# A three-stage pipeline over sixteen groups: the third stage four iterations behind the first instead of five, with a new order on every engine

## The chip, the core and the metric

The kernel runs on one core of a Trainium2 chip. The core has TensorE (PE, products and transposes), VectorE (DVE), ScalarE (ACT), GpSimd (POOL) and SyncE (SP, which issues DMAs). Each engine works through a list of its own in order, and semaphores tie the lists together. The metric is the device time of one execution in microseconds.

## What is computed

The input is 32 sequences of 256 tokens of 128 values. Three residual steps follow one another:

```python
    x = x + 0.5 * _L0_ffn_ref(_layernorm(x, axis=-1), ...)
    x = x + _L0_attn_ref(_layernorm(x, axis=-1), L0_attn_W_qkv, L0_attn_W_out)
    x = x + 0.5 * _L0_ffn_ref(_layernorm(x, axis=-1), ...)
```

The feed-forward is a mixture of eight experts (four of width 128, four of width 256). A router takes each token's two best by the sigmoid of its logits, weighs them to a sum of one, and the result is the weighted sum of `square(relu(x @ W1e)) @ W2e`. The attention is linear: `elu(q) + 1` and `elu(k) + 1` after a rotary embedding, 16 heads of 8, with one state per head and sequence:

```python
    kv = jnp.einsum('bhtd,bhtv->bhdv', k_feat, v)
    k_sum = k_feat.sum(axis=2)
    denom = jnp.maximum(jnp.einsum('bhtd,bhd->bht', q_feat, k_sum), 1e-06)
    out = jnp.einsum('bhtd,bhdv->bhtv', q_feat, kv) / denom[..., None]
```

## The kernel before, in words

**Groups, streams, chunks.** 16 groups (`NG`) of two sequences, 512 tokens each. Each group goes through three streams: `f1` (first feed-forward), `at` (attention), `f2` (second feed-forward). A feed-forward has 12 chunks (`NC`) of 128 hidden columns. A chunk is three products "up" on TensorE (`up`, L496 to L498; values are split into a high and a low part, so one product becomes three), then VectorE's relu times the root of the expert's weight (`weighted`, L1025, tile `hid`), ScalarE's square (L719) and rounded copy `h_hi` (L730), GpSimd's remainder `h_lo` (L858), and three products "down" (`down`, L514 to L516). "Up" writes two PSUM banks in turn; `hid` has six buffers.

**Iterations and places.** Every engine runs `iteration(t)` for t from -3. An iteration has 24 places. f1 of group t+1 takes places 0 to 11, one chunk each; f2 of group t+1-`SHIFT` takes places 12 to 23; a chunk's down products stand 9 places behind its up products (`DOWN_BEHIND`). Where one feed-forward is alone (`alone`), it takes every second place over 24. `SHIFT` is 5, so f1 is alone for t=-1 to 3 and f2 from the second half of t=14; between them the iterations are paired. `quarter(t, j)` on TensorE and `squares(t, j)` on ScalarE do the places 3j to 3j+2; `weighted(t, place)` on VectorE and `remainders(t, ...)` on GpSimd go by single places.

**What stands between the places.** Around the chunks each engine's `iteration` writes out by hand where the other steps go. For each stream: statistics (`stats`, `mean_variance`), the inverse deviation on GpSimd (`inv_std`), the normed input `xn` on ScalarE (`norm`, L676), its transpose on TensorE (`transpose`, L458) into PSUM bank 0, the evacuation to `xT` (`evacuate_x`, L688), high and low parts (`high_part` on VectorE, `low_part` on GpSimd, L846). `xT` is one buffer that all three streams share, and `evacuate_x` waits until the low parts of the others are made. The routers add `logits` (L477), `exp_logits` (L697, L701), the choice of two on VectorE, `root_of_weights` (L852) on GpSimd, `spread_roots` (L1003, L1009), `weight_rows` (L467, bank 0 again), `rows_of_weights` (`g_row`, L709), and SyncE's DMAs that write the rows to HBM and broadcast them into `g_all`, which `weighted` needs. `tp_free` makes TensorE wait until bank 0 is read. At a feed-forward's end ScalarE copies its sum (`copy_yT`, L741; it waits for the last down product), TensorE transposes it back (`back`, L533) and VectorE adds it to x (`add_moe`, L1033).

**Attention** is `q` and `kv` (L547), the rotary steps on VectorE (`rope_q_sin` L1044, `rope_q_cos`, `rope_q_sum`, `rope_k`, `rope_k_sum`), `exp_q`, `copy_v` (L762), `exp_k` on ScalarE, `q_features`, `k_features`, `state` (L589), `mask_state`, `attend` (L601), `normalise`, `attn_transpose` (L610), `copy_attnT` (L767), `out_proj` (L620) and `add_attention` (L1128). Before, iteration t did q and kv of group t-1 late and state to out_proj of group t-2.

Of the kernel before, what the change touches and what calls it, by code (L numbers as in the profile page):

```python
# [47 lines left out]
CQ = NC // TG  # L48
# [15 lines left out]
SHIFT = 5  # L64
# [103 lines left out]
def build(nc, x_in, wqkv, wout, router, w1, w2, const, out, rows):  # L168
    ctx = ExitStack()
    with ctx:  # L170
# [263 lines left out]
        def _(pe):  # L434
            mm = nc.tensor.matmul

            def tp_free(t, pos):

                n = [done(m + (pos > k)) for k, m in
                     enumerate((t + 2, t + 1 - SHIFT, t - 1, t + 2 - SHIFT, t + 2))]  # L440
# [4 lines left out]
                if due(n[2]):  # L445
                    pe.wait_ge(s_xT["at"], value(n[2]))
                if due(n[3]):
                    pe.wait_ge(s_ex["f2"], value(n[3]))
                if due(n[4]):
                    pe.wait_ge(s_gr["f1"], value(n[4]))  # L450
# [85 lines left out]
            def quarter(t, j, par):  # L536

                for place in range(CQ * j, CQ * (j + 1)):
# [86 lines left out]
            def iteration(t, par):  # L625
                transpose("f1", t + 2, t, 0)
                quarter(t, 0, par)
                state(t - 2)
                logits("f1", t + 2)
                quarter(t, 1, par)  # L630
                weight_rows("f2", t + 1 - SHIFT, t, 1)
                attend(t - 2)
                quarter(t, 2, par)
                transpose("at", t - 1, t, 2)
                quarter(t, 3, par)
                attn_transpose(t - 2)
                if alone("f1", t - 1):
                    back("f1", t, t - 1)
                if not alone("f2", t - 1):
                    back("f2", t - SHIFT, t - 1)  # L640
                transpose("f2", t + 2 - SHIFT, t, 3)
                quarter(t, 4, par)
                out_proj(t - 2)
                q(t - 1)
                logits("f2", t + 2 - SHIFT)
                quarter(t, 5, par)
                weight_rows("f1", t + 2, t, 4)
                quarter(t, 6, par)
                kv(t - 1, 0)
                kv(t - 1, 1)  # L650
                quarter(t, 7, par)
# [9 lines left out]
        def _(act):  # L661
# [17 lines left out]
            def evacuate_x(s, n, t, pos):  # L679
# [31 lines left out]
            def squares(t, j):  # L711

                todo = [k for place in range(CQ * j, CQ * (j + 1)) for k in chunks(t, place)]
# [57 lines left out]
            def iteration(t, par):  # L771
                n1, n2, n2_last = t + 1, t + 1 - SHIFT, t - SHIFT
                evacuate_x("f1", t + 2, t, 0)
                squares(t - 1, 7)
                norm("at", t - 1)
                exp_logits("f1", t + 2)
                squares(t, 0)
                norm("f2", t + 2 - SHIFT)
                squares(t, 1)
# [5 lines left out]
                evacuate_x("at", t - 1, t, 1)  # L785
# [452 lines left out]
```

## Time and profile before

| | us |
|---|---|
| median of 3 runs | 803.7 (803.64 to 804.73) |
| the profiled execution | 804.86 |
| its span in the trace | 803.1 |
| busy: TensorE / GpSimd | 725.4 / 686.8 |
| busy: ScalarE / VectorE | 598.4 / 582.8 |

The span is what the trace covers, from the first to the last instruction. Products overlap on TensorE and their ends are modelled, so its pace is read from starts. An idle time in brackets behind an instruction is that of its engine just before it, with what ended it.

### The profile page before, as it was taken

The numbers are of one execution on the slowest core, as the hardware profiler recorded it, in microseconds if no ns is written. First come the engines' busy times: TensorE is split into PE (matmuls) and PEld (weight loads), VectorE is DVE, ScalarE is ACT, GpSimd is POOL, SyncE is SP. The second block draws the span as 40 slices with busy tenths as digits, with TensorE's granted clock in tenths as the row PEclk, the third lists the DMA queues.
The fourth block names the chain that finished last, engine by engine and source line by source line (L and its number), as shares of the span: only waits on it lengthen the run. The fifth ranks groups of instructions, "written<-read, shape, count | busy, mean of one in ns | idle before, by whom it ended". The sixth has DMA issues, their size and how long they took to land.

```text
span 803.1 us, 13042 instructions
## 1 busy us (share of the span) xinstructions
PE 725.4 (90%) x3600; PEld 589.8 (73%) x3600; DVE 582.8 (73%) x1832; ACT 598.4 (75%) x1219; POOL 686.8 (86%) x668
## 2 busy tenths in 40 slices
PE   1779888889999999999999999999999987978987
PEld 1557666667788888888888888888887866866755
DVE  3445689787969787877878796978786768577533
ACT  3577677657787978888888888797878776656755
POOL 3778868869999999999999999999999868667865
PEclk9999899989999999999999999999999999899989
DMA  5544022033233221333323233322223311303330
GB/s 177 184 162 130 13 95 106 1 105 107 106 107 119 85 94 49 129 97 106 119 107 120 107 120 105 119 76 101 66 104 107 119 61 46 120 2 118 119 119 26
DMA packets 31159, 79.36 MB, mean 99 GB/s; under 512 B 3312, under 2 KB 14448, under 8 KB 31088
## 3 DMA queue, kind: packets, MB, share of 16 engines
q1 hardware_dynamic: 30800, 78.47, 28.9%
q8 instruction: 29, 0.48, 0.2%
q14 instruction: 42, 0.34, 0.1%
q10 hardware_dynamic: 288, 0.07, 0.1%
HBM read 73.81 MB, written 4.72 MB: 98 GB/s over the span
## 4 chain that ended last, share of the span: by engine, by line
POOL 39%; PE 21%; DVE 18%; issue 9%; ACT 8%; DMA 4%; DVEq 0%; POOLq 0%; SPq 0%; ACTq 0%
POOL h_lo L858 26%; DVE hid L1025 5%; POOL root_f L852 4%; DMA g_all_f<-rows_f 3%; PE bank L496 3%; PE bank L514 3%; POOL rstd_f L837 2%; PE bank L498 2%; PE bank L497 2%; PE bank L516 2%; PE bank L515 2%; ACT h_hi L730 2%; POOL x_lo_f L846 2%; ACT xn_f L676 2%; PE bank L589 2%
## 5 line engine op out<-in xcount | busy, mean ns | idle before, releaser
L858 POOL TENSOR_TENSOR h_lo<-hid,h_hi 128x512 fp32r<-128x512 f32 x384 | 493.5, 1311 | 79.1 <-ACT h_hi L730 78.7
L1025 DVE SCALAR_TENSOR_TENSOR hid<-bank,g_all_f 128x512 f32<-128x512 f32 x384 | 262.5, 685 | 151.3 <-PE bank L498 109.5
L719 ACT ACTIVATE hid<-hid 128x512 f32<-128x512 f32 x384 | 228.8, 622 | 52.0 <-DVE hid L1025 51.5
L730 ACT ACTIVATE h_hi<-hid 128x512 fp32r<-128x512 f32 x384 | 225.6, 620 | 4.9 <-ACT hid L719 0.8
L496 PE MATMUL bank<-x_hi_f,w_hi 128*128 128x512 f32 x384 | 166.8, 434 | 16.4 <-DVE hid L1025 15.8
L514 PE MATMUL bank<-h_hi,w_hi 128*128 128x512 f32 x384 | 156.7, 408 | 17.3 <-ACT yT L741 10.4
L498 PE MATMUL bank<-x_hi_f,w_lo 128*128 128x512 f32 x384 | 154.7, 403 | 0.0
L515 PE MATMUL bank<-h_lo,w_hi 128*128 128x512 f32 x384 | 154.0, 401 | 0.0
L497 PE MATMUL bank<-x_lo_f,w_hi 128*128 128x512 f32 x384 | 153.8, 401 | 0.0
L516 PE MATMUL bank<-h_hi,w_lo 128*128 128x512 f32 x384 | 153.6, 400 | 0.0
L496 PEld LDWEIGHTS bank<-x_hi_f,w_hi 128*128 128x128 f32 x384 | 74.4, 194 | 41.4 <-DVE hid L1025 24.9
L514 PEld LDWEIGHTS bank<-h_hi,w_hi 128*128 128x128 f32 x384 | 74.0, 193 | 39.8 <-POOL h_lo L858 14.0
L498 PEld LDWEIGHTS bank<-x_hi_f,w_lo 128*128 128x128 f32 x384 | 74.0, 193 | 18.2
L516 PEld LDWEIGHTS bank<-h_hi,w_lo 128*128 128x128 f32 x384 | 73.5, 191 | 17.1
L515 PEld LDWEIGHTS bank<-h_lo,w_hi 128*128 128x128 f32 x384 | 73.9, 192 | 16.1
L497 PEld LDWEIGHTS bank<-x_lo_f,w_hi 128*128 128x128 f32 x384 | 74.7, 195 | 11.1
L676 ACT ACTIVATE xn_f<-x_sb,nbias_f,rstd_f 128x128 f32<-128x128 f32 x128 | 52.4, 481 | 7.8 <-POOL nbias_f L839 7.8
L852 POOL TENSOR_TENSOR root_f<-cwt_f,c_half 128x8 f32<-128x8 f32 x32 | 54.6, 1706 | 0.0
L846 POOL TENSOR_TENSOR x_lo_f<-xT,x_hi_f 128x512 fp32r<-128x512 f32 x32 | 41.6, 1299 | 14.0 <-DVE x_hi_f L943 14.0
L688 ACT ACTIVATE xT<-bank 128x512 f32<-128x512 f32 x48 | 28.4, 591 | 29.0 <-PE bank L458 19.1
L943 DVE CAST x_hi_f<-xT 128x512 fp32r<-128x512 f32 x32 | 21.5, 671 | 26.8 <-ACT xT L688 26.8
L697 ACT ACTIVATE ex_f<-bank 128x32 f32<-128x32 f32 x32 | 6.3, 198 | 45.1 <-PE bank L477 45.1
(102 smaller groups left out, 1021.3 us busy)
## 6 DMA issues: line engine op xcount, KB each, us to landing
g_all_f<-rows_f SPq DMA_DIRECT2D x128, 512.0 KB, 5.5
x_sb<-in_x SPq DMA_DIRECT2D x16, 256.0 KB, 3.3
out_x<-x_sb SPq DMA_DIRECT2D x16, 256.0 KB, 7.1
g_all_f<-in_w SPq DMA_DIRECT2D x2, 768.0 KB, 6.8
con<-in_const SPq DMA_DIRECT2D x1, 584.0 KB, 6.4
rows_f<-g_row_f SPq DMA_DIRECT2D x32, 16.0 KB, 1.4
g_all_f<-in_wqkv SPq DMA_DIRECT2D x1, 192.0 KB, 6.5
con<-in_const ACTq DMA_DIRECT2D x1, 68.0 KB, 3.2
```

Source lines behind the costliest of these rows:

```text
L496: mm(o, w1_hi[:, w], x_hi[s][u][:], start=True, stop=False)
L497: mm(o, w1_hi[:, w], x_lo[s][u][:], start=False, stop=False)
L498: mm(o, w1_lo[:, w], x_hi[s][u][:], start=False, stop=True).then_inc(s_p1[s], 1)
L514: mm(o, w2_hi[:, c, :], h_hi[:, c, :], start=(c == 0), stop=False)
L515: mm(o, w2_hi[:, c, :], h_lo[:, c, :], start=False, stop=False)
L516: i = mm(o, w2_lo[:, c, :], h_hi[:, c, :], start=False, stop=(c == NC - 1))
L676: i = fn(xn[s][:, k, :], tile, ACT.Identity, bias=nbias[s][:, k:k + 1], scale=rstd[s][:, k:k + 1])
L719: fn(h, h, ACT.Square).then_inc(s_sq[s], 1)
L730: fn(h_hi[:, c, :], hid[:, c % STAGE, :], ACT.Copy).then_inc(s_hhi[s], 1)
L852: gp.tensor_tensor(root[s][:], cwt[s][:], c_half[:], ALU.pow).then_inc(s_root[s], 1)
L858: gp.tensor_tensor(h_lo[:, c, :], hid[:, c % STAGE, :], h_hi[:, c, :].bitcast(F32), ALU.subtract).then_inc(s_hlo[s], 1)
L1025: v.scalar_tensor_tensor(hid[:, c % STAGE, :], hp[c % 2][:], 0.0, g_all[s][:, EXPERT[c], :], ALU.max, ALU.mult).then_inc(s_z[s], 1)
```

## The change

`SHIFT` goes from 5 to 4. So f2 of a group starts one iteration sooner, and its router and the attention have to be through earlier: state, attend, normalise and attn_transpose are now done in iteration t for group t-1 (only out_proj stays with t-2), and the transpose of the attention's input for group t stands late in iteration t instead of in the middle of t+1. The steps between the places are set anew on TensorE, ScalarE, GpSimd and VectorE. `quarter(t, j)` becomes `places(t, a, b)`, `squares(t, j)` becomes `squares(t, a, b)`. The code has one line more from L62 on, up to four more further down.

```diff
-SHIFT = 5
+SHIFT = 4
...
             def iteration(t, par):
                 transpose("f1", t + 2, t, 0)
-                quarter(t, 0, par)
-                state(t - 2)
+                places(t, 0, 3, par)
+                out_proj(t - 2)
+                q(t - 1)
                 logits("f1", t + 2)
...
+                places(t, 14, 16, par)
+                state(t - 1)
                 transpose("f2", t + 2 - SHIFT, t, 3)
...
+                places(t, 16, 19, par)
+                attend(t - 1)
                 logits("f2", t + 2 - SHIFT)
...
+                places(t, 19, 22, par)
+                transpose("at", t, t, 4)
+                places(t, 22, 24, par)
+                attn_transpose(t - 1)
...
-                for q, m in (("f1", t + 2), ("at", t - 1), ("f2", t + 2 - SHIFT)):
-                    m = done(m + 1 if STREAMS.index(q) < pos else m)
+                for k, (q, m) in enumerate((("f1", t + 2), ("f2", t + 2 - SHIFT), ("at", t))):
+                    m = done(m + 1 if k < pos else m)
...
+                squares(t - 1, 21, 23)
+                evacuate_x("at", t - 1, t - 1, 2)
                 evacuate_x("f1", t + 2, t, 0)
-                squares(t - 1, 7)
-                norm("at", t - 1)
+                squares(t - 1, 23, 24)
+                copy_attnT(t - 2)
                 exp_logits("f1", t + 2)
...
+                squares(t, 14, 17)
+                evacuate_x("f2", t + 2 - SHIFT, t, 1)
                 if not alone("f1", t):
                     copy_yT("f1", n1, t)
...
-                squares(t, 6)
-                exp_q(t - 1)
-                copy_v(t - 1)
-                exp_k(t - 1)
+                squares(t, 17, 19)
+                exp_logits("f2", t + 2 - SHIFT)
+                squares(t, 19, 20)
+                norm("at", t)
+                squares(t, 20, 21)
```

How it moves the work shows in the engines' lists of a paired iteration. In the names, bank3 is the sum of f1, bank4 that of f2, bank0 the shared transpose bank.

ScalarE, before, from the first router's weight rows on: yT of f1 is followed by the squares of places 18 to 20 and the attention's exponentials.

```order
L709 ACTIVATE g_row_f1<-bank0,c_cut 32x128
L741 ACTIVATE yT<-bank3 128x512
L719 ACTIVATE hid<-hid 128x512 x2
L730 ACTIVATE h_hi<-hid 128x512
L719 ACTIVATE hid<-hid 128x512
L730 ACTIVATE h_hi<-hid 128x512 x2
L746 ACTIVATE eq<-bank5,c_mone 128x512
```

Behind that stand the copies of v, exp_k and the evacuation of f1's input. ScalarE in the changed kernel, from the second router's evacuation on:

```order
L689 ACTIVATE xT<-bank0 128x512
L742 ACTIVATE yT<-bank3 128x512
L720 ACTIVATE hid<-hid 128x512 x2
L731 ACTIVATE h_hi<-hid 128x512 x2
L698 ACTIVATE ex_f2<-bank0 128x32
L702 ACTIVATE odds_f2<-ex_f2,c_one 128x32
L720 ACTIVATE hid<-hid 128x512
L731 ACTIVATE h_hi<-hid 128x512
L677 ACTIVATE xn_at<-x_sb,nbias_at,rstd_at 128x128 x4
```

The norm of the attention, xn_at, moved from the start of the next iteration to a place behind yT and four steps.

TensorE in the changed kernel, from the last down product of f1 (place 20) through place 21 to the attention's transpose and the next up product:

```order
L516 MATMUL bank3<-h_hi,w2_lo 128x512
L496 MATMUL bank2<-x_hi_f20,w1_hi 128x512
L497 MATMUL bank2<-x_lo_f20,w1_hi 128x512
L498 MATMUL bank2<-x_hi_f20,w1_lo 128x512
L514 MATMUL bank4<-h_hi,w2_hi 128x512
L515 MATMUL bank4<-h_lo,w2_hi 128x512
L516 MATMUL bank4<-h_hi,w2_lo 128x512
L458 MATMUL bank0<-con,xn_at 128x128 x4
L496 MATMUL bank1<-x_hi_f20,w1_hi 128x512
```

Before, the same transpose stood behind place 8, ahead of the first down product of f1:

```order
L514 MATMUL bank4<-h_hi,w2_hi 128x512
L515 MATMUL bank4<-h_lo,w2_hi 128x512
L516 MATMUL bank4<-h_hi,w2_lo 128x512
L458 MATMUL bank0<-con,xn_at 128x128 x4
L496 MATMUL bank2<-x_hi_f11,w1_hi 128x512
```

One place of f2 is all that stands between the end of f1's sum and the attention's transpose now. Before, that transpose had no step of ScalarE's yT of f1 in the same iteration ahead of it.

GpSimd around the iteration's end, before; f1's low part stands behind place 22:

```order
L858 TENSOR_TENSOR h_lo<-hid,h_hi 128x512 x3
L846 TENSOR_TENSOR x_lo_f11<-xT,x_hi_f11 128x512
L858 TENSOR_TENSOR h_lo<-hid,h_hi 128x512 x3
L834 TENSOR_TENSOR ve_f1<-mv_f1,c_eps 128x4
L835 TENSOR_TENSOR nm_f1<-mv_f1,c_mone 128x4
```

and in the changed kernel, where the attention's low part stands behind place 22 and f1's behind place 23:

```order
L862 TENSOR_TENSOR h_lo<-hid,h_hi 128x512 [waits s_hhi_f2] x6
L850 TENSOR_TENSOR x_lo_at0<-xT,x_hi_at0 128x512 [waits s_hi_at]
L862 TENSOR_TENSOR h_lo<-hid,h_hi 128x512 [waits s_hhi_f2]
L856 TENSOR_TENSOR root_f2<-cwt_f2,c_half 128x8 [waits s_cwt_f2]
L850 TENSOR_TENSOR x_lo_f10<-xT,x_hi_f10 128x512 [waits s_hi_f1]
```

Two low parts, both made from the one buffer xT, now stand one remainder and one root apart.

## Rows read from the trace of the kernel before

**Rows 1.** The page: the span.
```profile
span 803.1 us, 13042 instructions
```
**Rows 2.** Windows: stretch, length, busy us of PE, PEld, DVE, ACT, POOL; PEclk, DMA, GB/s.
```profile
75.40:104.50 29.10, 23.41 (x101) 18.21 (x99) 20.89 (x63) 19.23 (x39) 22.33 (x23) 0.88 0.28 96
260.10:303.70 43.60, 43.31 (x226) 36.05 (x225) 35.41 (x116) 36.45 (x78) 43.07 (x42) 1.00 0.30 104
713.30:738.50 25.20, 24.12 (x116) 19.33 (x117) 15.91 (x53) 16.82 (x33) 14.52 (x13) 0.93 0.29 95
738.50:760.90 22.40, 18.68 (x88) 14.41 (x87) 12.17 (x37) 17.08 (x35) 19.78 (x20) 1.00 0.28 106
```
**Rows 3.** Timeline of TensorE, paired; last an alone iteration: start us, us, line.
```profile
276.09 0.39 PE L514 MATMUL bank<-h_hi,w_hi 128*128 128x512 f32 x1
276.32 0.40 PE L515 MATMUL bank<-h_lo,w_hi 128*128 128x512 f32 x1
...
277.49 0.39 PE L514 MATMUL bank<-h_hi,w_hi 128*128 128x512 f32 x1
...
305.89 1.05 PE L589 MATMUL bank<-v_sb,kf 128*128 128x129 f32 x8
...
307.59 0.48 PE L496 MATMUL bank<-x_hi_f,w_hi 128*128 128x512 f32 x1
...
338.00 0.40 PE L516 MATMUL bank<-h_hi,w_lo 128*128 128x512 f32 x1
...
343.84 0.60 PE L533 MATMUL bank<-con,yT 128*128 128x128 f32 x4
...
344.63 0.47 PE L496 MATMUL bank<-x_hi_f,w_hi 128*128 128x512 f32 x1
...
681.22 2.06 PE L589 MATMUL bank<-v_sb,kf 128*128 128x129 f32 x8 [3.37 <-DVE qf L1064]
```
**Rows 4.** Timeline of ScalarE, paired iterations and (last two rows) one f2-alone iteration.
```profile
305.69 1.64 ACT L676 ACTIVATE xn_at<-x_sb,nbias_at,rstd_at 128x128 f32<-128x128 f32 x4
307.85 0.20 ACT L697 ACTIVATE ex_f<-bank 128x32 f32<-128x32 f32 x1 [0.52 <-PE bank L477]
...
308.36 1.14 ACT L719 ACTIVATE hid<-hid 128x512 f32<-128x512 f32 x2
...
311.49 1.63 ACT L676 ACTIVATE xn_f<-x_sb,nbias_f,rstd_f 128x128 f32<-128x128 f32 x4
...
338.43 0.60 ACT L741 ACTIVATE yT<-bank 128x512 f32<-128x512 f32 x1 [1.33 <-PE bank L516]
338.92 1.14 ACT L719 ACTIVATE hid<-hid 128x512 f32<-128x512 f32 x2
...
342.05 0.67 ACT L746 ACTIVATE eq<-bank,c_mone 128x512 f32<-128x512 f32 x1
342.62 0.38 ACT L762 ACTIVATE v_sb<-bank 128x256 f32<-128x256 f32 x1
...
660.87 0.62 ACT L719 ACTIVATE hid<-hid 128x512 f32<-128x512 f32 x1
...
662.14 0.58 ACT L767 ACTIVATE attn<-bank 128x512 f32<-128x512 f32 x1
```
**Rows 5.** Timeline of VectorE, a paired iteration.
```profile
331.46 1.39 DVE L1044 TENSOR_TENSOR qb<-bank,con 64x512 f32<-64x512 f32 x2
...
333.75 0.81 DVE L926 BATCH_NORM_STATS2 bn_at<-x_sb 128x6 f32<-128x128 f32 x4
```
**Rows 6.** Waits in the window 260.1 to 303.7: us in total, times, longest.
```profile
ACT xT L688 <- POOL x_lo_at L846: 0.7, 1, 0.7
```
**Rows 7.** Windows, two stretches in f2-alone iterations; columns as in rows 2.
```profile
679.90:686.70 6.80, 5.48 (x17) 4.68 (x18) 3.49 (x8) 5.70 (x13) 3.94 (x4) 0.50 0.01 2
649.20:652.60 3.40, 3.40 (x13) 3.01 (x13) 1.89 (x5) 3.05 (x8) 1.09 (x2) 0.50 0.02 5
```
**Rows 8.** Waits in the window 27 to 56, two f1-alone iterations.
```profile
DVE hid L1025 <- DMA g_all_f<-rows_f: 10.8, 2, 5.9
```

More of the change, by code:

```diff
@@ L534, in back, with places @@
                 i.then_inc(s_y[s], 1)
-            def quarter(t, j, par):
-                for place in range(CQ * j, CQ * (j + 1)):
+            def places(t, a, b, par):
+                for place in range(a, b):
                     for s, n, c, ago in chunks(t, place):
@@ L626, in iteration @@
                 transpose("f1", t + 2, t, 0)
-                quarter(t, 0, par)
-                state(t - 2)
+                places(t, 0, 3, par)
+                out_proj(t - 2)
+                q(t - 1)
                 logits("f1", t + 2)
-                quarter(t, 1, par)
+                places(t, 3, 6, par)
                 weight_rows("f2", t + 1 - SHIFT, t, 1)
[L632 to L636, printed above, removed]
+                places(t, 6, 9, par)
+                kv(t - 1, 0)
+                kv(t - 1, 1)
+                places(t, 9, 12, par)
                 if alone("f1", t - 1):
@@ L640, in iteration @@
                     back("f2", t - SHIFT, t - 1)
+                places(t, 12, 14, par)
+                weight_rows("f1", t + 2, t, 2)
+                places(t, 14, 16, par)
+                state(t - 1)
                 transpose("f2", t + 2 - SHIFT, t, 3)
-                quarter(t, 4, par)
-                out_proj(t - 2)
-                q(t - 1)
+                places(t, 16, 19, par)
+                attend(t - 1)
                 logits("f2", t + 2 - SHIFT)
[L646 to L651, printed above, removed]
+                places(t, 19, 22, par)
+                transpose("at", t, t, 4)
+                places(t, 22, 24, par)
+                attn_transpose(t - 1)
                 if alone("f2", t - 1):
@@ L709, in rows_of_weights, with squares @@
                 fn(g_row[s][:], tp[0:EXP * TG, 0:P], ACT.Relu, bias=c_cut[0:EXP * TG, 0:1]).then_inc(s_gr[s], 1)
-            def squares(t, j):
-                todo = [k for place in range(CQ * j, CQ * (j + 1)) for k in chunks(t, place)]
+            def squares(t, a, b):
+                todo = [k for place in range(a, b) for k in chunks(t, place)]
                 for k in range(len(todo) + 1):
@@ L772, in iteration @@
                 n1, n2, n2_last = t + 1, t + 1 - SHIFT, t - SHIFT
+                squares(t - 1, 21, 23)
+                evacuate_x("at", t - 1, t - 1, 2)
                 evacuate_x("f1", t + 2, t, 0)
-                squares(t - 1, 7)
-                norm("at", t - 1)
+                squares(t - 1, 23, 24)
+                copy_attnT(t - 2)
                 exp_logits("f1", t + 2)
-                squares(t, 0)
-                norm("f2", t + 2 - SHIFT)
-                squares(t, 1)
+                squares(t, 0, 3)
+                squares(t, 3, 6)
                 rows_of_weights("f2", n2)
@@ L784, in iteration @@
                     copy_yT("f1", t, t - 1)
-                evacuate_x("at", t - 1, t, 1)
                 if not alone("f2", t - 1):
                     copy_yT("f2", n2_last, t)
-                squares(t, 2)
-                squares(t, 3)
-                copy_attnT(t - 2)
-                evacuate_x("f2", t + 2 - SHIFT, t, 2)
+                exp_q(t - 1)
+                squares(t, 6, 9)
                 if live(t - SHIFT):
                     norm("f1", t + 3)
-                exp_logits("f2", t + 2 - SHIFT)
-                squares(t, 4)
-                squares(t, 5)
+                squares(t, 9, 12)
+                copy_v(t - 1)
+                exp_k(t - 1)
+                norm("f2", t + 2 - SHIFT)
+                squares(t, 12, 14)
                 rows_of_weights("f1", t + 2)
@@ L1146, in iteration @@
                     add_moe("f1", t, t - 1)
+                spread_roots("f2", n2_last, 0)
                 weighted(t, 3)
+                spread_roots("f2", n2_last, 1)
+                rope_q_sin(t - 1)
                 stats("f1", t + 3, (par + 1) % 2)
```

86 lines of the change are left out of this document (40 added, 46 removed).

## The prediction

> **What bounds the kernel now.** I read the windows by iteration first, then the timelines of TensorE and ScalarE inside one iteration, then the waits. The windows [rows 2] are cut at the first chunk of each iteration. A paired iteration, one that does 12 chunks of each feed-forward, takes 43.6 us, and TensorE shows 43.31 of it busy, GpSimd 43.07. There are ten such iterations and the first half of an eleventh (t=4 to 14). Iterations with one feed-forward alone hold half the chunks but cost far more than half: 29.1 (t=1), 25.2 (t=17), 22.4 us (t=18).
>
> TensorE's floor in a paired iteration comes from its timeline [rows 3]. A place is six products of 512 columns; the L514 of one place starts at 276.09 and that of the next at 277.49, so 1.40 us, and 24 of them make 33.6. The small products stand in 8 clusters between places, the first from 305.89 to 307.59 (1.70), the last from 343.84 to 344.63 (0.79); all 8 sum to 8.9. Together 42.5, so 1.1 us of the 43.6 is slack. Whatever makes TensorE stand still for more than that lengthens the iteration.
>
> A page of the Trainium skill speaks against reading TensorE as full. "Perfetto Trace Analysis", Identifying the Most-Contended Engine, says that matmul busy time is a poor measure and weight-load busy time a good one. By that rule TensorE, with 36.05 us of weight loads in 43.6, has 7.5 us of room.
>
> I read against it, because the starts themselves are 0.23 us apart with no gap between them [rows 3], which is a rate and not a busy share. What the rule would give is the fourth rival.
>
> **Fewer iterations.** The second feed-forward starts one iteration earlier and ends one earlier. One first-alone iteration goes, the one like t=1 (29.1), and one second-alone iteration, the mean of t=17 and 18 (23.8); one paired iteration comes (43.6). Sum: 43.6 - 29.1 - 23.8 = -9.3, so 803.1 [rows 1] becomes 793.8 if no iteration changed its length. The work is the same; what goes is idle time.
>
> **The wait that comes: TensorE's attention transpose.** This is where I expect the loss. In the new order ScalarE does, one behind the other: copy yT of the first feed-forward, the squares of places 17 and 18, the exponentials of the second router, the square of place 19, and then the norm of the attention (xn_at). TensorE's transpose of that xn_at stands behind place 21. But yT needs the last down product of the first feed-forward, which is in place 20 (chunk 11, nine places behind). So ScalarE cannot begin this run before place 20 is through, and TensorE has only place 21 to do meanwhile.
>
> The run, by starts [rows 4]: yT to the next 0.49 (338.43 to 338.92). Two squares and two high parts, four at 0.52, 2.08 (six of them take 3.13 from 308.36 to 311.49). The exponentials 0.51 (307.85 to 308.36). A square done singly 1.27 (660.87 to 662.14), since its high part must wait for it. The norm 1.64 (305.69). Sum 5.99. In the old trace the last product of place 20 starts at 338.00 [rows 3] and yT at 338.43; the norm would end at 344.42, and with 0.1 for the semaphore the transpose could start at 344.5. TensorE would be there at 338.00 + 0.23 + 1.40 = 339.63. **Stall: 4.9 us per paired iteration.** ScalarE waits for that product already today, 1.33 us [rows 4], with one place of squares more in front and nothing urgent behind; it costs nothing because xn_at is then made elsewhere. I see nothing that can shorten the stall, as each engine runs its own list in order.
>
> **Smaller waits of the new order,** by the same rows. (a) Transpose of the second router's input: it overwrites the bank from which ScalarE has to fetch the first router's weight rows, and that fetch is now behind yT of the second feed-forward (which waits for place 8), exp_q, two runs of three squares, two norms, copy_v, exp_k and a pair: 0.49 + 0.57 + 3.13 x 2 + 1.54 x 2 + 1.3 + 2.08 + 0.34 = 14.1, TensorE's way there 12.7; stall about 1.6 with the product's tail, between 0 (if yT came earlier) and 2.5. (b) VectorE gets rope_q_sin (1.39 for its two halves) and the statistics (0.81) between places 3 and 4 [rows 5], then cos and sum behind 4 and 5; two up banks let it be 1.2 late, so about 1.0, from 0 to 2. (c) The two xT evacuations now stand one behind the other. The second waits for GpSimd's low part of the first, while the square that GpSimd needs next stands behind it on ScalarE. GpSimd idles 0.16 + 0.50 + 1.27 + 0.1, some 2.1 us; that alone would make a GpSimd-bound iteration 43.6 + 2.1 = 45.7, below what TensorE's stalls make, so I add none of it. Today that low part costs ScalarE 0.7 [rows 6]. Its effect on TensorE: transpose f1 waits 0.35 for the first evacuation, and out_proj 0.65 for attnT, which is copied behind the second. Together 1.0, from 0 to 2.5.
>
> So a paired iteration takes 42.5 + 4.9 + 1.6 + 1.0 + 1.0 = 51.0 us.
>
> **The clock.** TensorE waits 3.37 us until 681.22, and the stretch from 679.9 to 686.7 ran at a granted clock of 0.50, 1.2 GHz [rows 3, 7]. From 681.22 to 686.7 that loses half of 5.5, 2.7 us. From 649.2 to 652.6 it was the same after a wait that ended at 649.1: half of 3.4, 1.7. Paired iterations run at 1.00 today and would get such a wait each. Part of the low stretch will lie in the wait itself, and slower products hide the 1.0 of (c); I add 1.0, from 0 to 3. Paired iteration: **52.0 us, 8.4 more than now.**
>
> **The rest.** t=14 is paired in its first half and still has the long wait: +4. In the first-alone iterations the first router's weight rows move from behind place 17 to behind 13, about two chunks earlier; VectorE now waits there for the weights' DMA, 10.8 us in two waits [rows 8]. I take -2 for each of two iterations, -4 (0 to -10). At the end the second router starts at place 16 instead of 12 and must be through by place 12 of the next: +1.5 for each of two, +3 (0 to +6). The SP queue's issues keep their order.
>
> Sum: 793.8 + 11 x 8.4 + 4 - 4 + 3 = 889.2 us of span. The profiled execution took 804.86 and the median is 803.7, 0.6 above its span, so 890.
>
> **Rivals.**
> 1. Only the transpose's wait counts. (a) to (c) and the clock's loss lie in slack or in that wait: 42.5 + 4.9 = 47.4, +3.8 each, 793.8 + 42 + 1 = 837; with half of the others 860. For it: a longer iteration gives every other chain more time. Against: (a) is a separate loop, from place 8 to the transpose behind 15. 18%.
> 2. The new waits aren't there, the paired iteration stays at 43.6, and the time is 794, faster. It would be so if ScalarE reached xn_at by the time of place 21; it decides at a paired iteration of 44.5, where the 9.3 saved are used up (9.3/11 = 0.85 each). 6%.
> 3. Only GpSimd's handshake counts: 45.7, 794 + 23 = 817. 4%.
> 4. TensorE has the room that its weight loads leave: 36.05 + 8.5 = 44.6, 794 + 11 = 805, about as before. This is the page's rule as a mechanism; the starts of 0.23 speak against it. 3%.
> 5. It gets worse: two low stretches of the clock per iteration, and squares so late that GpSimd starves too: 55 us or more, 925 and up. 7%.
> The forecast, paired iterations of 49.5 to 55, 861 to 925: 62%.
>
> Range 837 to 925, which holds the forecast and the first rival, 80%. Differences under 0.2% (1.6 us) can't be told from no change. Faster: 0.06, most of rival 2. Within: 0.02, part of rival 4. Slower: 0.92.
>
> **What will show it.** Right: the paired windows are 50 to 54 us; the longest repeated wait of TensorE is the attention transpose's (L458, on ACT xn_at), near 4.9 us, twelve times; ScalarE's yT waits 3 us or more for TensorE; the page's clock line falls below 9 in the middle slices; GpSimd's busy share falls from 85% to about 77%. (a) shows as a wait of the f2 transpose for ACT g_row. Wrong: no wait on xn_at beyond 2 us, or paired windows under 45 us. If the middle is 52 and the total isn't near 890, the alone iterations are what I mis-sized.

## The result, and the profile after

The changed kernel takes 910.1 us (median of 4 runs, 907.98 to 910.88) against 803.7 before: ratio 1.132, 95% interval 1.129 to 1.134. The prediction was 890, range 837 to 925.

A note on line numbers: TensorE's lines are the same in both kernels, ScalarE's and VectorE's stand one further down in the changed one (L741 is L742, L1025 is L1026), GpSimd's four (L858 is L862).

The page of the changed kernel: span, busy times with their shares of the span, and TensorE's granted clock in 40 slices (in tenths).

```profile
span 907.6 us, 13088 instructions
PE 758.1 (84%) x3600; PEld 605.8 (67%) x3600; DVE 591.3 (65%) x1832; ACT 601.5 (66%) x1219; POOL 687.9 (76%) x668
...
PEclk9999899999989899998999999998999989899999
```

The work is that of before. GpSimd is busy for 687.9 us, before 686.8, so the 104.5 us added are all idle time of GpSimd's; its share is 76%, foretold as about 77%. TensorE shows 32.7 us more busy time than before for the same 3600 instructions, in part because more of them ran at half clock (98.2 us at about 0.50, before 43.3). The clock line has an 8 in many of the middle slices, as foretold. Two groups of the page carry the new idle time (busy, mean ns of one, then the idle time in front of them):

```profile
L742 ACT ACTIVATE yT<-bank 128x512 f32<-128x512 f32 x32 | 19.0, 594 | 84.5 <-PE bank L516 84.5
L458 PE MATMUL bank<-con,xn_at 128*128 128x128 f32 x64 | 16.3, 403 | 63.9 <-ACT xn_at L677 63.9
```

Windows over a first-alone iteration (t=1), two paired ones (t=6 and 7) and t=14, to compare with [rows 2]:

```profile
81.50:118.70 37.20, 29.00 (x130) 23.26 (x130) 24.19 (x70) 21.17 (x42) 22.64 (x24) 0.87 0.15 58
315.50:367.80 52.30, 45.86 (x227) 37.19 (x226) 36.55 (x115) 36.75 (x76) 42.12 (x42) 0.97 0.22 87
367.80:421.60 53.80, 47.04 (x227) 37.73 (x226) 37.37 (x114) 36.74 (x76) 43.13 (x42) 0.94 0.25 85
738.60:781.40 42.80, 39.52 (x193) 33.00 (x192) 28.11 (x79) 28.17 (x57) 31.84 (x31) 0.92 0.17 56
```

A paired iteration takes 52.3 or 53.8 where it took 43.6, and one with the first feed-forward alone takes 37.2 where the one that stood there took 29.1. Inside the paired iteration from 367.8, the waits (us in total, times, longest; `issue` is a pause for which the trace names no releaser):

```profile
POOL h_lo L862 <- ACT h_hi L731: 8.8, 6, 2.1
...
ACT yT L742 <- PE bank L516: 6.4, 2, 5.2
...
PE bank L458 <- ACT xn_at L677: 4.7, 1, 4.7
...
ACT xT L689 <- POOL x_lo_at L850: 3.2, 1, 3.2
...
PE bank L496 <- issue: 0.7, 1, 0.7
PE bank L458 <- ACT g_row_f L710: 0.7, 1, 0.7
PE bank L496 <- DVE hid L1026: 0.4, 1, 0.4
PE bank L620 <- ACT attn L768: 0.3, 1, 0.3
```

ScalarE's timeline shows the run that the prediction had put together from rows of before [rows 4]:

```profile
407.54 0.60 ACT L742 ACTIVATE yT<-bank 128x512 f32<-128x512 f32 x1 [5.16 <-PE bank L516]
408.04 1.14 ACT L720 ACTIVATE hid<-hid 128x512 f32<-128x512 f32 x2
409.08 1.14 ACT L731 ACTIVATE h_hi<-hid 128x512 fp32r<-128x512 f32 x2
410.12 0.18 ACT L698 ACTIVATE ex_f<-bank 128x32 f32<-128x32 f32 x1
...
411.88 1.63 ACT L677 ACTIVATE xn_at<-x_sb,nbias_at,rstd_at 128x128 f32<-128x128 f32 x4
```

and TensorE's, the transpose that waits for its end:

```profile
407.11 0.39 PE L516 MATMUL bank<-h_hi,w_lo 128*128 128x512 f32 x1
...
408.51 0.40 PE L516 MATMUL bank<-h_hi,w_lo 128*128 128x512 f32 x1
...
413.57 1.11 PE L458 MATMUL bank<-con,xn_at 128*128 128x128 f32 x4 [4.66 <-ACT xn_at L677]
```

The last product of place 20 starts at 407.11, yT can start at 407.54, and the transpose starts 6.46 us behind the product. One place (to 408.51) is all that TensorE had for that time.

**Where the 104.5 us of span came from.** By the length of each iteration (from its first relu to the next iteration's), with what the prediction's sum gave the same stretch:

| stretch (t of the changed kernel) | before | in the sum | measured | over the sum |
|---|---|---|---|---|
| up to the first relu | 26.8 | 26.8 | 25.9 | -0.9 |
| t=-1 to 2, first feed-forward alone (before: to 3) | 144.1 | 111.0 | 131.3 | +20.3 |
| t=3 to 13, eleven paired (before: ten, 4 to 13) | 437.9 | 573.9 | 581.4 | +7.5 |
| t=14 | 40.1 | 44.1 | 42.8 | -1.3 |
| t=15 to the end | 154.2 | 133.4 | 126.2 | -7.2 |
| span | 803.1 | 889.2 | 907.6 | +18.4 |

The eleventh paired iteration replaces a first-alone one of 29.1 and a second-alone one. Had each paired iteration kept its 43.6, the middle would be 481.5; it is 99.9 longer. Against the 793.8 us that the exchange of iterations alone would give, the span is 113.8 longer: 99.9 of that is the middle, 16.3 the iterations with the first feed-forward alone (131.3 against 115.0), and the rest of the kernel gives 2.4 back.

### The profile page after: what moved, and what is told of

Its sections match the earlier page's. It is cut to its first block, busy times and chain, and to the rows that moved or that the text cites. A ratio compares the mean times of both kernels' runs of the same rounds, so it can differ in the third digit from the quotient of the medians.

```text
span 907.6 us, 13088 instructions
## 1 busy us (share of the span) xinstructions
PE 758.1 (84%) x3600; PEld 605.8 (67%) x3600; DVE 591.3 (65%) x1832; ACT 601.5 (66%) x1219; POOL 687.9 (76%) x668
## 4 chain that ended last, share of the span: by engine, by line
PE 36%; ACT 27%; POOL 13%; DVE 11%; issue 10%; DMA 2%; ACTq 0%; DVEq 0%; POOLq 0%; SPq 0%
ACT h_hi L731 7%; ACT hid L720 6%; POOL h_lo L862 6%; PE bank L496 5%; PE bank L498 5%; PE bank L497 5%; ACT xn_f L677 4%; PE bank L514 4%; PE bank L516 4%; PE bank L515 4%; DVE hid L1026 4%; POOL root_f L856 3%; PE bank L458 3%; ACT xn_at L677 3%; PE bank L477 2%
## 5 line engine op out<-in xcount | busy, mean ns | idle before, releaser
L862 POOL TENSOR_TENSOR h_lo<-hid,h_hi 128x512 fp32r<-128x512 f32 x384 | 495.2, 1312 | 172.2 <-ACT h_hi L731 172.1
L1026 DVE SCALAR_TENSOR_TENSOR hid<-bank,g_all_f 128x512 f32<-128x512 f32 x384 | 260.7, 681 | 200.7 <-PE bank L498 154.3
L720 ACT ACTIVATE hid<-hid 128x512 f32<-128x512 f32 x384 | 231.7, 623 | 98.1 <-DVE hid L1026 97.5
L496 PE MATMUL bank<-x_hi_f,w_hi 128*128 128x512 f32 x384 | 174.3, 454 | 15.8 <-DVE hid L1026 9.2
L497 PE MATMUL bank<-x_lo_f,w_hi 128*128 128x512 f32 x384 | 158.5, 413 | 0.0
L498 PE MATMUL bank<-x_hi_f,w_lo 128*128 128x512 f32 x384 | 158.3, 412 | 0.0
L515 PE MATMUL bank<-h_lo,w_hi 128*128 128x512 f32 x384 | 156.9, 408 | 0.0
L496 PEld LDWEIGHTS bank<-x_hi_f,w_hi 128*128 128x128 f32 x384 | 77.4, 202 | 46.3 <-DVE hid L1026 21.5
L497 PEld LDWEIGHTS bank<-x_lo_f,w_hi 128*128 128x128 f32 x384 | 77.7, 202 | 9.9
L742 ACT ACTIVATE yT<-bank 128x512 f32<-128x512 f32 x32 | 19.0, 594 | 84.5 <-PE bank L516 84.5
L458 PE MATMUL bank<-con,xn_at 128*128 128x128 f32 x64 | 16.3, 403 | 63.9 <-ACT xn_at L677 63.9
L458 PEld LDWEIGHTS bank<-con,xn_at 128*128 128x128 f32 x64 | 10.4, 199 | 70.8 <-ACT xn_at L677 70.8
```

Of the source, the lines that this page charges most:

```text
L496: mm(o, w1_hi[:, w], x_hi[s][u][:], start=True, stop=False)
L497: mm(o, w1_hi[:, w], x_lo[s][u][:], start=False, stop=False)
L498: mm(o, w1_lo[:, w], x_hi[s][u][:], start=False, stop=True).then_inc(s_p1[s], 1)
L515: mm(o, w2_hi[:, c, :], h_lo[:, c, :], start=False, stop=False)
L720: fn(h, h, ACT.Square).then_inc(s_sq[s], 1)
L862: gp.tensor_tensor(h_lo[:, c, :], hid[:, c % STAGE, :], h_hi[:, c, :].bitcast(F32), ALU.subtract).then_inc(s_hlo[s], 1)
```

## The experiments

The theory: the transpose's wait for xn_at makes over half of the loss, because yT and the squares stand ahead of the norm on ScalarE; the other engines' waits are hidden beside it, GpSimd's handshake over xT among them, and come out once it is gone. The rivals: the transpose's place on TensorE is at fault; the handshake is; the clock is. Four kernels, each the changed one with one edit.

**x1_yT_last**: the copy of yT behind the norm.

```diff
-                if not alone("f1", t):
-                    copy_yT("f1", n1, t)
                 squares(t, 17, 19)
                 exp_logits("f2", t + 2 - SHIFT)
                 squares(t, 19, 20)
                 norm("at", t)
+                if not alone("f1", t):
+                    copy_yT("f1", n1, t)
                 squares(t, 20, 21)
```

> The changed kernel with one step of ScalarE moved: in paired iterations the copy of yT of the first feed-forward stands behind xn_at instead of four steps ahead of it. Theory (the order yT before xn_at makes TensorE's transpose wait, and that wait brings the low clock): the wait on xn_at, 4.7 us today in each of twelve iterations, falls below 1; the low stretches of the middle go; paired iterations fall from 52.9 to 45.5 to 47.5, where GpSimd's and ScalarE's remaining waits bound them; total 825 to 850. Rival (ScalarE's list as a whole bounds the iteration, and the wait only shows there): the wait turns up at another step of TensorE, paired iterations stay above 51, total above 885.

Measured: 849.5 us, ratio 1.058 (1.054 to 1.061); a paired iteration 48.1, the transpose's wait 0.5. The total lies at the upper end of what I expected, the iteration 0.6 above it. So 60.7 us of the 106 lost hang on where one copy of 0.6 us stands. The order "yT before the norm" was not needed by any data: xn_at doesn't read yT. What mainly holds the 48.1 now is GpSimd: of the chain of work that ended last (from the last instruction back, at each step to what released it), some 60% is GpSimd's in a paired iteration, and the rest passes through the other three engines at its waits. Its timeline of one iteration:

```profile
352.85 1.27 POOL L862 TENSOR_TENSOR h_lo<-hid,h_hi 128x512 fp32r<-128x512 f32 x1 [2.06 <-ACT h_hi L731]
...
358.32 2.55 POOL L862 TENSOR_TENSOR h_lo<-hid,h_hi 128x512 fp32r<-128x512 f32 x2 [1.36 <-ACT h_hi L731]
...
361.27 0.20 POOL L838 TENSOR_TENSOR ve_f<-mv_f,c_eps 128x4 f32<-128x4 f32 x1 [0.40 <-DVE mv_f L936]
...
368.40 1.30 POOL L862 TENSOR_TENSOR h_lo<-hid,h_hi 128x512 fp32r<-128x512 f32 x1 [0.40 <-ACT h_hi L731]
...
385.77 0.20 POOL L838 TENSOR_TENSOR ve_at<-mv_at,c_eps 128x4 f32<-128x4 f32 x1 [0.65 <-DVE mv_at L936]
```

These waits sum to 4.87; with the 42.86 that the window shows of GpSimd's work that is 47.7 of the 48.1. Such a sum proves nothing by itself, as TensorE's busy time and waits, 44.85 and 3.3, give 48.2 as well; but each of TensorE's listed waits is 0.8 or less.

**x2_transpose_late**: the transpose of the attention behind place 23 on TensorE.

```diff
-                transpose("at", t, t, 4)
                 places(t, 22, 24, par)
+                transpose("at", t, t, 4)
```

> The changed kernel with one step of TensorE moved: the attention's transpose stands behind place 23 instead of behind 21, so that two places of work (2.8 us) fill its wait. Theory: the wait falls from 4.7 to about 1.9 us and the low clock comes in fewer iterations or none; some of it comes back, as the evacuation behind it comes later: paired iterations 48.5 to 51, total 860 to 888. Rival (GpSimd's waits bound the paired iteration, not TensorE's): total within 5 us of 910.

Measured: 886.2 us, ratio 1.103 (1.100 to 1.107); paired 51.4 mostly, 52.9 now and then. Two places more of cover (2.8 us) take the wait for xn_at to 0.2 and give back 24 us in all, some 1.6 per paired iteration, less than their length: the evacuation comes later as well, the next transpose waits 2.4 for xT, and an up product waits 1.4 for `hid`. More than half of the 1.6 is the clock's, which stayed at 1.00 in most of these iterations: set against x3 below, which has 52.1 at full clock, the cover itself is worth 0.7. To cover the run from the other side is worth less than to shorten it.

**x3_fill_wait**: 18 products of 512 columns ahead of the transpose (some 4.2 us of TensorE), so that the engine doesn't stand still while it waits. Their results are overwritten and used by nothing.

```diff
+                fill(t, par)
                 transpose("at", t, t, 4)
```

> The changed kernel with 18 products of 512 columns added on TensorE just ahead of the attention's transpose, in iterations with both feed-forwards; they write a PSUM bank that the next place overwrites and feed nothing. At 0.23 us each they take 4.2 us of the wait of 4.7. This measures the clock's part alone. Theory: the granted clock of the paired iterations is 1.00, and each gets 1.5 to 2 us shorter, 51 instead of 52.9; total 885 to 893. Rival (the low stretches lie in slack): same total as the changed kernel, 910, or more by what the added products take.

Measured: 896.4 us, ratio 1.116 (1.113 to 1.120). The window over a paired iteration, and below it the waits in it:

```profile
363.40:415.50 52.10, 48.91 (x245) 39.19 (x244) 37.73 (x114) 36.77 (x76) 42.97 (x42) 1.00 0.28 87
```

```profile
PE bank L458 <- ACT g_row_f L720: 0.7, 1, 0.7
PE bank L629 <- ACT attn L778: 0.7, 1, 0.7
...
PE bank L458 <- ACT xn_at L687: 0.5, 1, 0.5
```

The clock is at 1.00 and the full paired iterations (t=4 to 12) are 52.1 to 52.3, none 53.8. So the clock's price in the changed kernel is 53.05 - 52.1 = 0.95 per paired iteration where the two kinds take turns, 1.2 over all eleven (581.4 against 568.6 us), and 13.7 us in all. That is near the prediction's 1.0 and less than the 1.5 to 2 that I had come to expect by the time of this run, and the total is above the 885 to 893 expected. The changed kernel had 98.2 us at about 0.50 and this one 40.7; 57.5 us at half clock cost 13.7 and not the 29 that half of them would be. Part of them lies in the wait itself, and part of the gain goes into other waits: with full clock the output product waits 0.7 for attnT where it waited 0.3.

**x4_square_first**: the evacuation of f1's input behind the square of place 23, so that GpSimd has a remainder to do while ScalarE waits for the low part.

```diff
-                evacuate_x("f1", t + 2, t, 0)
                 squares(t - 1, 23, 24)
+                evacuate_x("f1", t + 2, t, 0)
```

> The changed kernel with ScalarE's evacuation of the first feed-forward's input moved behind the square of place 23, so that GpSimd's remainder of place 23 needn't wait for it. Theory: this handshake has slack as long as the longer wait on xn_at stands: paired iterations change by less than 0.7 us, total 898 to 912. Rival (the handshake is on the path): 2.1 us less in each of twelve iterations, total near 883.

Measured: 907.3 us, ratio 1.130 (1.126 to 1.134); paired 53.3 and 52.3. The intervals of the two ratios overlap, so it can't be told from the change. Alone the handshake costs nothing that shows, as the prediction had it.

**y1_both**: x1 and x4 together.

> x1_yT_last and x4_square_first together. x1 alone has paired iterations of 48.1 us, in which GpSimd works 43.2 and waits 4.9: 2.06 for the high part of place 23, 1.36 for that of place 0, three times 0.40 to 0.65 elsewhere. Theory (paired iterations are bound by GpSimd now, and the shared buffer xT causes the first wait): the 2.06 goes but half of it comes back as a longer second wait, since the exponentials that stand ahead of place 0's squares come only 1.2 us earlier: paired 46.7 to 47.2, total 833 to 840. Rival (TensorE's own waits bound it): no change from x1, 849.

Measured: 838.3 us, ratio 1.042 (1.038 to 1.046); paired 46.9. The same edit that brought 3 us at most in x4 now brings 11: what was hidden counts once the other wait has gone. GpSimd's waits per iteration are now 2.18, 0.65, 0.40 and 0.35. The handshake (low part of the attention, evacuation, square of place 23, its remainder) stands on x1's chain and no longer on this one. But neither does GpSimd mainly hold the iteration any more: the chain spends 12.8 us on TensorE, 12.8 on GpSimd, 10.6 on ScalarE, 4.2 on VectorE and the rest in hand-overs. Among its links are the statistics of f1 and the attention's mean and variance on VectorE, and yT of f2 on ScalarE.

**y2_ex_late**: y1 and, on ScalarE, attnT ahead of the evacuation and the first router's exponentials behind the squares of places 0 to 2.

```diff
-                evacuate_x("f1", t + 2, t, 0)
                 copy_attnT(t - 2)
-                exp_logits("f1", t + 2)
+                evacuate_x("f1", t + 2, t, 0)
                 squares(t, 0, 3)
+                exp_logits("f1", t + 2)
```

> y1_both and, on ScalarE, attnT copied ahead of the evacuation of f1's input and the first router's exponentials moved behind the squares of places 0 to 2. Theory: both GpSimd waits at the iteration's start are gone (3.4 us): paired 44.5 to 45.3, total 808 to 818. Rival (GpSimd then waits elsewhere as much, or TensorE's waits take over): above 46, total above 825.

Measured: 836.9 us, ratio 1.040 (1.035 to 1.045); paired 47.0, so my expectation was wrong and the rival right. GpSimd's 2.18 us in front of the remainder of place 0 went, and came back at the statistics, which VectorE delivers late. The chain says why nothing was won: it is that of y1, with 12.8 us each on TensorE and GpSimd, 10.6 on ScalarE and 4.2 on VectorE, and neither f1's exponentials nor attnT stands on it; the wait that I removed was slack.

```profile
POOL ve_f L838 <- DVE mv_f L936: 2.5, 1, 2.5
POOL ve_at L838 <- DVE mv_at L936: 0.7, 1, 0.7
```

**y3_evac_first**: x1 and the attention's evacuation ahead of the squares of places 21 and 22.

```diff
-                squares(t - 1, 21, 23)
                 evacuate_x("at", t - 1, t - 1, 2)
+                squares(t - 1, 21, 23)
```

> x1_yT_last with ScalarE's evacuation of the attention's input moved ahead of the squares of places 21 and 22. It is meant for the three iterations with the first feed-forward alone (t=0 to 2), which take 107.1 us in the changed kernel where my sum had 88: there TensorE waits 1.7 to 2.1 us for this evacuation. Theory (the two transposes' waits are what I left out): each of the three gets 1.5 to 2.5 us shorter, 4 to 8 together, total 841 to 846 against 849. Rival (these iterations are bound by the router's chain, the transposes' waits lie in its slack): under 1.5 us together.

Measured: 850.2 us, ratio 1.057 (1.052 to 1.062), no change in the total. The mechanism was right at its place, and the edit also acts elsewhere: t=0 to 2 fell from 107.3 to 100.6, as TensorE's waits for xT went (2.1 in t=0), with 3.4 us less at half clock; but t=15, where f2 is alone, rose from 32.3 to 37.0. There GpSimd waits 12.5 us for ScalarE's high parts instead of 8.1, behind the squares that now come later. z1 below undoes the edit there.

**y5_more**: y2, y3's edit, and three more that answer the waits of y2: VectorE's statistics of f1 ahead of the root spreads and their mean and variance ahead of the first rope step, the attention's mean and variance ahead of f2's high part (not in the lines below), and yT of f2 behind the squares of places 6 to 8. All three are links of the chain of y1 and y2.

```diff
+                stats("f1", t + 3, (par + 1) % 2)
                 spread_roots("f2", n2_last, 0)
                 weighted(t, 3)
                 spread_roots("f2", n2_last, 1)
+                mean_variance("f1", t + 3)
                 rope_q_sin(t - 1)
-                stats("f1", t + 3, (par + 1) % 2)
...
-                if not alone("f2", t - 1):
-                    copy_yT("f2", n2_last, t)
                 exp_q(t - 1)
                 squares(t, 6, 9)
+                if not alone("f2", t - 1):
+                    copy_yT("f2", n2_last, t)
```

> All of x1, x4, y2 and y3 and, besides, on VectorE the statistics of f1 ahead of the first wait for root_f and the attention's mean and variance ahead of the high part of f2; on ScalarE yT of the second feed-forward behind the squares of places 6 to 8. Every wait of GpSimd in x1's paired iteration has its cause moved. Theory: paired iterations of 43.6 to 44.3 as in the kernel before, alone iterations as in y3, total 788 to 803, at or below the kernel before. Rival (four iterations' distance leaves too little time for the chains): paired stays above 45.5, total above 812.

Measured: 820.6 us, ratio 1.020 (1.016 to 1.025); paired 46.0. Wrong again in size: I had expected under 803. Now it is ScalarE that has no pause from 349.2 to 360.4, and f2's transpose waits at its end:

```profile
350.25 0.58 ACT L742 ACTIVATE yT<-bank 128x512 f32<-128x512 f32 x1
350.73 1.65 ACT L677 ACTIVATE xn_f<-x_sb,nbias_f,rstd_f 128x128 f32<-128x128 f32 x4
...
356.54 1.66 ACT L677 ACTIVATE xn_f<-x_sb,nbias_f,rstd_f 128x128 f32<-128x128 f32 x4
...
360.17 0.34 ACT L710 ACTIVATE g_row_f<-bank,c_cut 32x128 f32<-32x128 f32 x1
```

```profile
360.91 0.63 PE L458 MATMUL bank<-con,xn_f 128*128 128x128 f32 x4 [1.28 <-ACT g_row_f L710]
```

The first of the two norms is that of group t+3, wanted by TensorE at 376.24, at the next iteration's start and 25.5 us later. It stands on the chain of y5.

**z1_norm_moved**: y5 with that norm behind f2's evacuation, and y3's edit only up to t=14.

```diff
                 if not alone("f2", t - 1):
                     copy_yT("f2", n2_last, t)
-                if live(t - SHIFT):
-                    norm("f1", t + 3)
...
                 squares(t, 14, 17)
                 evacuate_x("f2", t + 2 - SHIFT, t, 1)
+                if live(t - SHIFT):
+                    norm("f1", t + 3)
```

> The kernel y5_more with two edits on ScalarE: the normalization of f1 of t+3, whose result is only wanted at the start of the next iteration, goes from behind the squares of places 6 to 8 to behind the evacuation of f2's transpose, and from t = 15 on (first router alone gone, second alone) the evacuation of the attention group's transpose stays behind squares 21 and 22. Theory (y5_more was bound by ScalarE's unbroken run between the squares of place 8 and the rows of weights of f1, which ended in a 1.28 us wait of f2's transpose and a 1.2 us wait for exp_k): those waits go, 0.6 to 1.7 us of the 46.0 of a paired iteration are won, so 44.3 to 45.4 each; t = 15 falls back from 34.8 to about 32.3; in all 11 x (0.6 to 1.7) + 2.5 = 9 to 21 less than 820.6, so 799 to 812. Rival (the second feed-forward's and attention's work per paired iteration leaves no engine in order enough room: the wait only goes to another of the same list): paired 45.5 or more, total over 813.

Measured: 806.2 us, ratio 1.0043 (1.0028 to 1.0058); paired 44.5, t=15 at 32.5. The theory held. A window over a paired iteration, and the waits of GpSimd and TensorE in one:

```profile
372.40:417.00 44.60, 43.90 (x227) 35.97 (x226) 35.26 (x115) 36.76 (x77) 43.10 (x42) 1.00 0.28 102
```

```profile
POOL h_lo L866 <- ACT h_hi L731: 1.1, 2, 0.7
...
PE bank L458 <- ACT xn_at L677: 0.5, 1, 0.5
```

With the same arrangement of streams as the change, some 103 of the 106 us have gone. It still isn't faster than before: the interval lies above 1. Set against before with its iterations exchanged (the 793.8 of the prediction), the tail is 5.1 us shorter and the start and t=14 1.0, but 8.4 are lost while the first feed-forward is alone (123.4 against 115.0) and 7.3 in the middle (488.8 against 481.5): 803.4, and the 9.3 are used up.

**z2_yT_f2_first**: z1 with yT of f2 back ahead of the squares of places 6 to 8.

> z1_norm_moved with the copy of yT of f2 back ahead of the squares of places 6 to 8, as the change has it. With the normalization gone from this stretch, ScalarE has the room either way. Theory: within 0.3 us of z1_norm_moved in a paired iteration (total within 4 us). Rival (the copy there makes ScalarE wait on TensorE's last bank of y, as it did in y1_both, and the squares of places 6 to 8 behind it come late for GpSimd's remainders): 0.5 to 1.5 us more in each of 11, total 5 to 16 above z1_norm_moved.

Measured: 813.5 us, ratio 1.012 (1.011 to 1.014), 7.3 over z1; paired 45.3. The rival: ScalarE has room for the copy's 0.5 us but not for the wait for TensorE in front of it, 1.26 us in a paired iteration, where z1 has none.

**w1_rows_later** and **w2_rows_and_at_later**: z1 with other places while the first feed-forward is alone, for the weight rows of f1 and ScalarE's fetch of them (both), and for the attention's transpose (w2, not in the lines below).

```diff
+                if live(t + 2 - SHIFT):
+                    weight_rows("f1", t + 2, t, 2)
...
+                if not live(t + 2 - SHIFT):
+                    places(t, 16, 18, par)
+                    weight_rows("f1", t + 2, t, 2)
+                    places(t, 18, 19, par)
```

> z1_norm_moved, but while the first router runs alone (t up to 1) the transposition of f1's weights stands behind place 17 on TensorE and behind the squares of places 14 to 16 on ScalarE, instead of behind place 13 and places 12 and 13. In z1_norm_moved TensorE waits there for g_tok 4.6, 2.3 and 3.9 us. Theory (these iterations are longer than before's because the transposition now stands ahead of data that VectorE makes only later): the waits mostly go, t = -1, 0 and 1 come down by 5 to 9 us together from 24.3 + 29.3 + 34.5, total 797 to 801.5, under the kernel before. Rival (the later broadcast only makes VectorE wait for g_all of f1 instead, as in the kernel before): less than 3 us won, total 803 to 807.

> w1_rows_later, and while the second feed-forward hasn't begun (t up to 2) attention's transpose stands behind place 23 instead of place 21 on TensorE, with its evacuation behind the squares of places 21 and 22. In z1_norm_moved TensorE waits there for xn_at 3.3, 2.1 and 1.3 us. Theory: 2 to 5 us less than w1_rows_later. Rival (the same chain, yT of f1 then first-router squares then the normalization, ends no earlier, and the evacuation now comes after more squares): within 2 us of w1_rows_later, or slower.

Measured: w1 802.7 us, ratio 0.9995 (0.998 to 1.001); w2 804.3, ratio 1.001 (0.999 to 1.003). Both can't be told from before. w1 took 2.6 us off t=-1 to 2, at the edge between theory and rival. In its iteration t=0 the wait for g_tok (2.3 in z1) is gone. That for xn_at is still there (3.3 in z1), that for yT has grown (2.5 in z1), and VectorE waits for a DMA, which it didn't in z1:

```profile
PE bank L514 <- ACT yT L748: 3.7, 1, 3.7
PE bank L458 <- ACT xn_at L683: 3.2, 1, 3.2
```

```profile
DVE hid L1039 <- DMA g_all_f<-rows_f: 4.0, 1, 4.0
```

That DMA is the rival's mechanism, the broadcast of the weights, as [rows 8] of before. In w2 the transpose waits less for xn_at (1.8) and the next one 2.4 for xT: no gain. No kernel of this study is shown to beat the one before.

## Why the prediction was right, and where it was off

**Floor and pace.** The prediction took TensorE for what holds the 43.6 of before. The trace says GpSimd: the chain of work that ended last, in the window 260.1 to 303.7, is GpSimd's from end to end (start us, us, what). It stands still for 0.08 and less at a time there, 0.53 in all. In four of the ten paired iterations that is so, and in the others TensorE has at most 17 us of the chain.

```profile
286.44 1.27 POOL x_lo_f L846
287.70 6.29 POOL h_lo L858 x5
...
295.67 3.79 POOL h_lo L858 x3
```

TensorE has little room beside it: its one listed wait there is 0.3, and 0.45 counted from start to start. So what the forecast needed, that a stall of TensorE of more than some 1 us lengthens the iteration, holds, as x1 shows; but the sum of 42.5 was 1.1 below what before itself reaches, and adding waits to 42.5 rather than to 43.6 is one reason for the shortfall below. The fourth rival, room by the weight loads' busy time (805), is 105 us off; the waits of the change and not that measure decided, so the time alone doesn't refute the measure. No run settles it: z1 even has the rival's 44.6 and 805, but its chain runs through GpSimd (12.9 us), TensorE (12.1), ScalarE (7.5) and VectorE (6.1), so no one engine's room set it.

**Fewer iterations, -9.3.** Right in kind, and too small at the end. The second-alone iteration that dropped out was worth 28, not the mean of two, 23.8: what ends the kernel (t=15 to 18) now takes 33.1, 29.1, 26.3 and 20.6, and before the five were 32.2, 32.2, 25.2, 22.4 and 25.2. The +3 for a later second router didn't come either. Together -7.2.

**The transpose's wait, 4.9.** Measured 4.66 in this iteration, 63.9 over the run in 16 waits: the eleven of the paired iterations at 4.6 to 4.7, and five from 1.6 to 3.3 before and behind them, where I had said twelve alike (that of t=14 is 3.3). The run of 5.99 took 5.97 (407.54 to the end of xn_at at 413.51). yT waits 5.16, foretold as 3 or more. x1 shows that it is the cause: without it the loss falls by 57%. The iteration falls by 53.05 - 48.1 = 4.95, the clock's loss among it, though by then GpSimd mainly holds it.

**(a) f2's transpose, 1.6.** It is there, on g_row as said, but 0.7. The same quantity is 0.7 in x1, and 1.28 in y5 where yT of f2 is later. **(b) VectorE, 1.0.** TensorE's wait for hid is 0.4. **(c) 1.0.** In the change 0.3 at out_proj and none at f1's transpose; with full clock (x3) 0.7 and 0.2, near the 0.65 and 0.35. So (a) to (c) are 1.4 against 3.6, while the whole, 52.85 on average over the eleven (53.05 in the middle ones), is over the 52.0. Counted from the 43.6 of before, 4.66, 1.4 and the clock's 1.2 make 50.9, and 2.0 are left. Some of it is in the trace. TensorE pauses 0.73 ahead of the up product at 390.55, the `issue` of the waits above, which no term of the prediction has. And a pause read from one start to the next is 0.16 to 0.17 longer than the one listed, since the modelled end of the product in front covers that much: 0.8 over five pauses. Some 0.5 stays open.

**The clock, 1.0.** Borne out: 0.95 to 1.2 by x3. From t=5 to 11 stretches of 6.8 and 3.4 us at 0.51 take turns, and the iterations, cut at their first relu, read 53.8 and 52.3 in turn. Cut from one transpose of xn_at to the next they are 53.1 on average behind a short stretch and 53.2 behind a long one, so the long one hardly costs more: 1.0 and 1.1 over x3.

```profile
412.00:418.80 6.80, 5.23 (x15) 4.27 (x16) 2.14 (x17) 5.19 (x11) 3.55 (x4) 0.51 0.01 2
360.80:364.20 3.40, 3.40 (x11) 2.82 (x11) 1.25 (x11) 1.97 (x4) 1.28 (x1) 0.51 0.00 0
```

**GpSimd's handshake, not added.** Right by x4; ScalarE waits 3.2 for the low part, and taking GpSimd's work out of that wait changes nothing that shows. Once it counted, y1 showed a price of 1.2 (48.1 less 46.9) where the third rival had 2.1. But there are other waits of that kind, on VectorE's statistics and on the squares, that the prediction didn't cost; without TensorE's long wait the iteration is 48.1 and not 45.7.

**The first-alone iterations, -4. This is the step that failed.** The prediction took f1's earlier weight rows for a gain of 2 us in each of two, and costed the new order's waits only in paired iterations and t=14. But the same transposes stand in the same places there, and the chains behind them are no shorter. TensorE's waits in t=0 and in t=1:

```profile
PE bank L514 <- ACT yT L742: 3.7, 1, 3.7
PE bank L458 <- ACT xn_at L677: 3.3, 1, 3.3
PE bank L458 <- ACT xT L689: 2.1, 1, 2.1
PE bank L467 <- DVE g_tok_f L1010: 0.8, 1, 0.8
```

```profile
PE bank L467 <- DVE g_tok_f L1010: 2.4, 1, 2.4
PE bank L458 <- ACT xn_at L677: 2.1, 1, 2.1
PE bank L514 <- ACT yT L742: 1.9, 1, 1.9
PE bank L458 <- ACT xT L689: 1.7, 1, 1.7
```

Of these before had only the wait for yT, 3.7. VectorE's waits for a DMA, 4.9 us in t=0 and 3.6 in t=1 before, have gone, as foretold; TensorE's waits stand in their stead. The 20.3 us over the sum are the 4 that didn't come and 16.3 of loss, all of it in t=0 to 2 (31.4, 37.2 and 38.5 us; t=-1 takes 24.2 as before, though TensorE waits 4.7 for g_tok there). The runs split it in part: without the wait for xT 6.7 go (y3), without that for g_tok 2.6 (w1 against z1). w1 is still 5.7 over 115.0 there, with waits for xn_at and yT left in it, and what each of these costs stays open. The prediction's last sentence named these iterations as what would be off if the middle was right.

That the total came within 2.3% is luck in part: the smaller waits were put 2.2 too high per paired iteration and the base 1.1 too low with 2 us uncosted, and the end of the kernel took back 7.2 of the 20.3.

**Rivals.** The first (837 to 860) didn't come: a paired iteration is 52.9 and not 47.4, so with the transpose's wait others do add, and the start of the pipeline besides. The decision point of the second, a paired iteration of 44.5, can be set against z1, which has 44.5 and comes out 0.4% slower than before, as the first-alone iterations ate 8.4.

## What to carry to other kernels

When steps are re-ordered in in-order lists, cost for each engine the run between what it waits for and what is waited for behind it, and ask of each step in that run whether the waiter reads it: here one 0.6 us copy stood ahead of a norm that doesn't need it, and cost 60 us. A wait that is removed shows the next one, so price the whole chain of lists, not one wait, and look before an edit whether its step stands on the chain that ended last: y5 and z1 moved steps of that chain and won 16 and 14 us, while y2 removed 2.2 us of waiting per iteration that wasn't on it, and won nothing. The list of waits alone doesn't tell the two apart. Cost a new order in every phase of a pipeline, its start and end too, since the same hand-overs stand there with less work to cover them.

## What the runs showed of the hardware that I had not expected

With the same wait of 4.7 us TensorE's granted clock is at 0.51 for 3.4 us in one iteration and for 6.8 us in the next, in turn from t=5 to 11, though the iterations issue the same work; at both ends of the middle long ones follow each other. And the price is small: 57.5 us more at half clock cost 13.7 us of time (the changed kernel against x3). Nor does the longer stretch cost twice as much: the transpose of xn_at at 466.87 goes with a stretch of 3.4 us, the one at 520.01 with one of 6.8, and the next transpose comes 53.14 us later both times.
